# Four units instead of two in a turn of the loops of three engines, in a Fourier block kernel

## What is computed

```python
xf = jnp.fft.rfft2(x, axes=(1, 2), norm='ortho').reshape(B, H, W // 2 + 1, 8, 96)
xr, xi = xf.real, xf.imag
o1r = relu(einsum(xr, w1[0]) - einsum(xi, w1[1]) + b1[0])
o1i = relu(einsum(xi, w1[0]) + einsum(xr, w1[1]) + b1[1])
o2r = einsum(o1r, w2[0]) - einsum(o1i, w2[1]) + b2[0]
o2i = einsum(o1i, w2[0]) + einsum(o1r, w2[1]) + b2[1]
o = softshrink(stack([o2r, o2i], axis=-1), 0.01)
out = irfft2(complex(o[..., 0], o[..., 1]), s=(H, W), norm='ortho') + x
```

## Time and profile before

| | |
|---|---|
| median of 3 executions | 5582.09 us (5570.92, 5582.09, 5591.25) |
| the profiled execution's own time | 5591.15 us |
| its span, from first to last instruction | 5589.4 us |
| granted TensorE clock, mean over the span | 0.982 of full speed |
| TensorE matmuls busy (PE) | 5320.8 us, 95% |
| TensorE weight loads busy (PEld) | 4981.4 us, 89% |
| ScalarE busy (ACT) | 3188.8 us, 57% |
| VectorE busy (DVE) | 3141.2 us, 56% |
| GpSimd busy (POOL) | 1252.8 us, 22% |

### The profile page before, as it was taken

One profiled execution on the slowest core, in us unless ns is written; L12 is line 12 of the kernel. 1 busy time (PEld: TensorE's weight loads), 2 busy tenths in 40 slices (PEclk: granted clock), 3 DMA queues, 4 the chain that ended last, 5 costly groups with the idle time before them and its releaser, 6 DMA issues.

```text
span 5589.4 us, 110666 instructions
## 1 busy us (share of the span) xinstructions
PE 5320.8 (95%) x42112; PEld 4981.4 (89%) x42112; DVE 3141.2 (56%) x5010; ACT 3188.8 (57%) x5744; POOL 1252.8 (22%) x810
## 2 busy tenths in 40 slices
PE   8999999999999999999999999999999999999997
PEld 8989889898898988989889898898998889988897
DVE  4556555565455564555645556455564555655555
ACT  5555565555665556655566555665555655556554
POOL 2211222112222022220222202222012221122200
PEclk9999999999999999999999999999999999999999
DMA  3331233321333213332133331333312333123311
GB/s 103 96 94 38 61 96 96 94 47 51 96 96 96 50 47 96 95 96 71 39 83 96 96 77 38 78 96 96 88 38 66 95 96 92 40 61 95 96 46 46
DMA packets 1131597, 429.79 MB, mean 77 GB/s; under 512 B 1130784, under 2 KB 1130912, under 8 KB 1131040
## 3 DMA queue, kind: packets, MB, share of 16 engines
q1 hardware_dynamic: 1131040, 422.23, 30.3%
HBM read 220.82 MB, written 201.33 MB: 76 GB/s over the span
## 4 chain that ended last, share of the span: by engine, by line
PE 94%; DVE 2%; issue 2%; ACT 2%; DMA 0%; DVEq 0%; SPq 0%; ACTq 0%
PE psum L525 17%; PE psum L561 14%; PE psum L538 13%; PE psum L582 12%; PE psum L607 12%; PE psum L592 8%; PE psum L547 7%; PE psum L619 3%; PE psum L620 3%; PE psum L621 3%; DVE mixed L461 1%; DVE x L491 1%; PE psum L579 0%; PE psum L599 0%; PE psum L598 0%
## 5 line engine op out<-in xcount | busy, mean ns | idle before, releaser
L461 DVE COPY mixed<-psum 128x768 f32<-128x768 f32 (+1 forms) x544 | 508.2, 934 | 1887.3 <-PE psum L547 1887.3
L318 POOL TENSOR_TENSOR doubled<-x 128x768 f32<-128x768 f32 x248 | 358.6, 1446 | 4024.1 <-DMA x<-x 4004.0
L525 PE MATMUL psum<-mats,x 128*96 128x128 f32 x8192 | 942.9, 279 | 65.7 <-issue 48.7
L525 PEld LDWEIGHTS psum<-mats,x 128*96 128x96 f32 x8192 | 931.0, 168 | 75.6 <-issue 55.2
L538 PE MATMUL psum<-w_whole,whole 128*128 128x192 f32 x4160 | 802.6, 336 | 113.8 <-ACT whole L357 68.8
L410 ACT ACTIVATE sums_high<-psum 128x512 fp32r<-128x512 f32 x768 | 459.8, 599 | 765.1 <-PE psum L607 765.1
L561 PEld LDWEIGHTS psum<-mats,mixed 128*128 128x128 f32 x6272 | 742.1, 191 | 119.6 <-issue 119.6
L561 PE MATMUL psum<-mats,mixed 128*128 128x128 f32 x6272 | 845.8, 284 | 0.0
L607 PE MATMUL psum<-mats,spectrum 128*128 128x128 f32 x6144 | 803.4, 276 | 26.4 <-DVE spectrum L467 26.4
L538 PEld LDWEIGHTS psum<-w_whole,whole 128*128 128x128 f32 x4160 | 688.9, 200 | 139.3 <-ACT whole L357 75.7
L582 PE MATMUL psum<-w2t,hidden 128*128 128x192 f32 x4160 | 771.9, 328 | 32.8 <-ACT hidden L401 32.2
(11 more groups left out here) (62 smaller groups left out, 6395.1 us busy)
## 6 DMA issues: line engine op xcount, KB each, us to landing
x<-x SPq DMA_DIRECT2D x160, 768.0 KB, 7.1
out<-x SPq DMA_DIRECT2D x160, 768.0 KB, 8.2
x<-x SPq DMA_DIRECT2D x32, 1488.0 KB, 10.5
out<-x SPq DMA_DIRECT2D x32, 1488.0 KB, 10.6
x<-x SPq DMA_DIRECT2D x32, 816.0 KB, 5.0
out<-x SPq DMA_DIRECT2D x32, 816.0 KB, 4.5
w2t<-L_conv_w SPq DMA_DIRECT2D x128, 36.0 KB
w_halved<-L_conv_w SPq DMA_DIRECT2D x128, 24.0 KB
```

The costliest lines, as they stand in the source:

```text
L461: dve.tensor_copy(mixed[s % 2][:, 0:k], both_b[:, 0:k]).then_inc(b_copied, 1)
L525: last = pe.matmul(bank_a(at)[:, i * SIZE:(i + 1) * SIZE], xs[par][:, slot, :], mat(FW_EVEN if slot <= HALF else FW_ODD), start=True, stop ...
```

## The change

The loops of TensorE, ScalarE and VectorE get a body of four units in place of two, and run 8 turns in place of 16. The index of the pair is now worked out from the loop's register, `m = loop * UNROLL + unit // 2`. On TensorE the two groups of stage A that are done ahead are now done for three of four units: all but the one at the head of the body. The loops of SyncE and GpSimd stay as they are.

```diff
         PAIRS = UNITS // 2
+
+        UNROLL = 2
...
-            with act.Fori(0, PAIRS) as m:
-                for par in range(2):
+            with act.Fori(0, PAIRS // UNROLL) as loop:
+                for unit in range(2 * UNROLL):
+                    m, par = loop * UNROLL + unit // 2, unit % 2
                     n = m * 2 + par
...
-            with dve.Fori(0, PAIRS) as m:
-                for par in range(2):
+            with dve.Fori(0, PAIRS // UNROLL) as loop:
+                for unit in range(2 * UNROLL):
+                    m, par = loop * UNROLL + unit // 2, unit % 2
                     n = m * 2 + par
...
-            with pe.Fori(0, PAIRS) as m:
-                for par in range(2):
+            with pe.Fori(0, PAIRS // UNROLL) as loop:
+                for unit in range(2 * UNROLL):
+                    m, par = loop * UNROLL + unit // 2, unit % 2
                     n = m * 2 + par
-                    stage_a(m, par, n, AHEAD * par, NA)
+                    stage_a(m, par, n, AHEAD if unit else 0, NA)
...
-                    if par == 0:
-
-                        stage_a(m, 1, n + 1, 0, AHEAD)
+                    if unit + 1 < 2 * UNROLL:
+                        stage_a(m + par, 1 - par, n + 1, 0, AHEAD)
```

## The result

The changed kernel takes 5540.72 us, the median of 5 executions (5532.61 to 5542.99); the kernel before took 5589.68 us in 5 executions beside it. The ratio is 0.992, with a 95% interval of 0.991 to 0.993: 0.8% faster, forecast 0.65%. The predicted time was 5546 us.

What follows compares the result with a forecast made beforehand. TensorE, busy 95% of the span, was taken to bound the kernel. From the 5582.1 us median, 43.6 saved on long stretches and 7.9 added for low clock gave 5546 us (0.65% less), range 5530 to 5562.

Steps and rivals of the forecast that it cites:

- The eight long stretches: Stage F's end to the mark, across back edges that go: 1419.8 us before, 1371.3 forecast, 48.5 saved.
- the mark: Cut point in stage A, after the pause for VectorE's last additions, where the 232 matmuls start.
- The groups ahead, 0.02 us where there were none: Stage A groups done before stage E cost 0.02 us a unit, hidden by a 1.65 us wait already there.
- The low clock, +7.9 us: TensorE's half-clock stretches land elsewhere: 3 more of 24 short units take 171.69 us, not 169.05, net of gains.
- The bounds: Low-clock range: 63 us more if all 24 short units are dear; gain side 36 us at full clock in stage B.
- the seven edges that stayed: Remaining TensorE back edges keep gaps between 3.19 and 3.35 us; 1 us either way.
- the 48.4 of the sum: Saving from the profiled execution before low clock: 48.5 us on long stretches, less 0.2 for groups ahead, rounded up.
- The base: Starting time: median 5582.09 us, not the profiled 5591.15; a median execution's eight stretches 4.8 us cheaper.
- Covers: Other engines' work stays hidden at boundaries: x ready 48 us early, weights 14 us before stage B.
- Rival 1: Only the edge gaps are won, low clock returns in stage B, C or E: 26 us, 5556 us; chance 0.22.
- Rival 2: Low clock in stages B and E becomes the rule: 2.64 us a unit, 5602 us with all 24; chance 0.04.
- Rival 3: Gap belongs to the first stage A on x0, moves into the body; 13 us saved, 5569 us; chance 0.06.

Runs made afterwards that it cites:

- experiment 1: Changed kernel with four units a turn, but groups ahead only for the second and fourth unit, as before: 5563.68 us, ratio 0.9965 to the kernel before.
- 10: Kernel before with eight unused matmul calls per unit filling TensorE's wait for ScalarE's gather ahead of stage B: 5552.81 us, ratio 0.9935.
- experiment 8: Changed kernel with only TensorE's loop at four units a turn, ScalarE's and VectorE's left at two: 5541.52 us, ratio 0.9933 to the kernel before.
- experiment 3: Kernel before with eight unused matmuls once ahead of TensorE's loop, shifting the loop head: 5599.45 us, ratio 1.0034.
- 6: Kernel before with groups ahead for every unit, last pair behind the loop, and prefetch hint on TensorE's back edge, head not placed: 5567.04 us, ratio 0.997.
- 7: Kernel before with groups ahead for every unit, last pair behind the loop, prefetch hint, and TensorE's loop head placed by padding: 5500.54 us, ratio 0.9835.
- experiment 9: Changed kernel with eight unused matmul calls per unit between stages A and B, in TensorE's wait for the gather: 5495.07 us, ratio 0.985 to the kernel before.

## Why the prediction was right

- **The eight long stretches** were forecast at 1371.3 us and took 1368.5 (48.5 us saved by forecast, 51.3 measured). The form came out as said: 16 matmuls ahead, 232 after the mark, 7 edges of 3.3 us.
- **The groups ahead, 0.02 us where there were none:** right on the clean clock (167.5 us from the mark to the end of stage F with them and without). Undervalued in effect: the wait they fill not only takes 1.65 us but brings about a low clock in some units (experiments 1 and 10), and I priced only its length.
- **The low clock, +7.9 us, was the mis-sized term.** I took three more of the 24 short units at 171.69. Seven of the 24 were dear in this sense or nearly, against two of 16 before, but eight ran at full clock throughout, which none of the 16 did. Full clock in stage B was worth 1.6 us a unit (169.1 - 167.5), against the estimate of 1.5. In the second and fourth units the two cancel (7.7 gained, 7.8 lost), and with the 2.8 us of the long stretches the term was a gain of 2.7 us in the trace and not a loss of 7.9. The bounds held this gain; the value chosen didn't. Beside it the seven edges that stayed became 6.5 us cheaper, mostly by one dear stretch instead of three, which I had left as it was. With 0.9 us at the start this is the whole way from the forecast for the profiled execution, 5550.6, to its 5532.6. Part of it is the luck of that fast execution: the medians are 49.0 us apart, which is the 48.4 of the sum with nothing for the low clock.
- **The base:** I put the profiled execution at the top of the range and let a median one save 43.6 us of 5582.1. The two further executions took 5590.96 and 5589.68 us, so the profiled one was ordinary and the correction from 48.4 to 43.6 had no ground.
- **Luck in the number.** The forecast saving was 5582.1 - 5546.4 = 35.7 us; measured are 49 us by the medians and 44 (37 to 51) by the ratio, so it was too small by some 8 to 13 us. The base was 7.6 us too low. The two errors go against each other, and the time came out within 6 us.
- **Covers:** all held. No wait for x or for a copy at a boundary appears; ScalarE's and VectorE's edges were worth nothing (experiment 8); the seven gaps with the longer body are 3.27 us on the mean.
- **Rivals.** Rival 1, that only the gap is won, is wrong for the change but describes its first half: experiment 1 won 16 us (12 to 27) where the gaps sum to 26, and the low clock came back in stage E. Rival 2 had its mechanism (stages B and E after a wait) but not its size. Rival 3 is out: the gap went with the edge, and with the hint.
- **The cited rule** of 108 ns for a compare-and-branch ("Advanced Engine Details and Errata", Control Flow Timing, in the Trainium skill) prices none of these edges: the trace has 3.25 us, and the difference is what the hint took away. With hint and place the edge left no wait that the profile lists, so no run here can show the 108 ns.

## What to carry to other kernels

Where a loop has a long body, look at its back edge for an "issue" gap: here a hint with the head well placed removed it without a longer body, and code put ahead of a loop can cost a microsecond per turn by shifting the head. On TensorE price a wait of 2 us at more than its length, because matmuls after it may run at half clock; unused matmuls inside such a wait can pay, as they did here. How many such slow stretches a trace shows shifted with every change made here, so leave room for it on both sides. And compare more than one execution before calling the profiled one fast or slow.

## What the hardware showed that I had not expected

- Shifting the loop head by eight matmul calls took the gap at an edge from 3.25 to 4.3 us, with the same body (experiment 3).
- The hint left 3.2 us of a gap of 4.3 on a badly placed head and nothing on a good one (6 and 7).
- Adding 256 unused matmul calls made the kernel 46 us faster, and the spread of five executions fell from 10 us to 1.6 (experiment 9).
- With neither edges nor the gather's wait, the granted clock is 0.998 over the span, and five executions lie within 0.5 us.
